# A graph-network edge stage on one core: its indirect gathers written out one by one, with the indices read in place

## The chip, the cores and the metric

One core of one Trainium2 chip runs the whole kernel in a single launch. The metric is the device time of a run in microseconds (us); the time before is the median of three runs. A profiled execution gives the instruction times that are read below. Engines are named as in the profile: PE (TensorE matmul), PEld (its weight load), DVE (VectorE), ACT (ScalarE), POOL (GpSimd), SP (SyncE, here the issuer of the plain DMAs).

## What is computed

Four graph layers over 1250 nodes of 512 features, with 21,250 edges sorted by their destination. Each layer's result is added to its input and layer-normalised. The first three use only sums over neighbours, which the kernel turns into products with a 1250 x 1250 matrix of edge counts. The fourth needs a message for each edge, and is the one that the change touches:

```python
def _L3_gnn_ref(x, edge_index, edge_attr, W1, b1, W2, b2, gamma, beta):
    src, dst = (edge_index[0], edge_index[1])
    msg = jax.nn.relu(x[src] + edge_attr)
    agg = jax.ops.segment_sum(msg, dst, num_segments=x.shape[0])
    h = x + agg
    h = jax.nn.relu(h @ W1 + b1) @ W2 + b2
    h = x + h
    mean = h.mean(axis=0)
    var = h.var(axis=0)
    h = (h - mean) * jax.lax.rsqrt(var + BN_EPS) * gamma + beta
    return h
...
x = _layernorm(x + _L3_gnn_ref(x, edge_index, edge_attr_512, ...), axis=-1)
```

## The kernel before

The program is one block per engine, with every wait written by hand as a semaphore count. Its stages follow each other: index preparation and counts (to about 120 us of the span), the three count-matrix layers (to about 380 us), the edge stage (380 to about 709 us), the second matrix of the last layer with batch norm, and the last layer norm with the store.

In the edge stage the edges are cut into `NG` = 42 groups of 512. A group is four edges (`TPG`) on each of 128 partitions. Groups are numbered g; rings of buffers hold them: `RING` = 6 slots of edge attributes (`ea`, 1 MB each) and `XRING` = 3 slots of gathered node rows (`xg`, also 1 MB). The program is seven rounds (`ITERS`) of six groups; round 0 is written out, later rounds are a hardware loop on the engines. For one group:

- **SP** loads 1 MB of attributes into `ea` (L355) once the scatter of the group six back has freed the slot; the first six loads are issued ahead (L330).
- **POOL** gathers the source rows. `gather` (L463 to L472) waits until the add of the group three back has freed the slot of `xg`, copies the group's 128 x 4 indices from the table `srcT_i` into a staging tile `idx4` (L467), waits for that copy, and issues four indirect DMAs (L471). Each of these fetches 128 rows of 2 KB from `x3_dram`, at the row numbers that stand in one column of the staging tile, into one quarter of the slot. The trace names the staging tile `idx` and the DRAM tensor `x_dram`.
- **DVE** adds, when the four gathers and the attributes have landed: `ea += xg` (L978), 128 x 2048 floats, both inputs in SBUF, and builds the one-hot window `hot_w` (L981). Every third group it adds a finished join into `preT` (L998), and once a round a block (L1005).
- **ACT** rectifies `ea` in place (L636), later copies the scatter's result to `zn` (L644) and the turned result to `zg` (L652).
- **PE** multiplies the one-hot window with the rectified rows (the scatter, L1311), transposes the result of the group before (the turn, L1322), and multiplies three groups at a time with the layer's first matrix (the join, L1332) or does a piece of the same product for the nodes themselves (the pre-block, L1296).

The table `srcT_i` (128 partitions x 42 x 4, int32, in SBUF) is written once by DVE at the start of the program, ahead of the count `idx_ready`, and never after. Ahead of the stage POOL waits for the stores of `x3_dram` and reads a flag; for irregular graphs it takes another path (L446 to L460), which these inputs don't take. Behind the stage, the last join must be added before ACT can rectify `preT` (L681) and PE can multiply with the second matrix (L1369).

The wait that frees a slot and the copy:

```python
if not (isinstance(g, int) and g < XRING):
    pool.wait_ge(add_done, g - XRING + 1)
pool.tensor_copy(idx4[:, slot, :], srcT_i[:, bass.ds(g, 1), :].rearrange("p a b -> p (a b)")).then_inc(idx_staged, 1)
pool.wait_ge(idx_staged, g + 1)
```

Of the kernel before, what the change touches and what calls it, by code (L numbers as in the profile page):

```python
# [37 lines left out]
NG = (E + GE - 1) // GE  # L38
# [9 lines left out]
RING = 6  # L48
# [4 lines left out]
XRING = 3  # L53
ITERS = NG // RING
# [14 lines left out]
def gnn_kernel(nc, x, src, dst, edge_attr, w01, b01, w02, b02, w11, b11, w12, b12, w2, b2,  # L69
               w31, b31, w32, b32, gamma, beta, out, x3_dram):  # L70
    with ExitStack() as ctx:
# [11 lines left out]
        def sb(name, shape, dtype):  # L83
            size = 2 if dtype in (BF16, F16) else 4
            n = 1
            for s in shape[1:]:
                n *= s
            return at(name, shape, dtype, place(n * size))

        def sem(name):  # L90
            return ctx.enter_context(nc.semaphore(name))
# [30 lines left out]
        a = r_a  # L122
# [7 lines left out]
        a = max(a, r_a + (KC * N * 4 + 2 * CH * 4 + 31) // 32 * 32)  # L130
# [63 lines left out]
        srcT_i = sb("srcT_i", [P, NG, TPG], I32)  # L194
        idx4 = sb("idx4", [P, XRING, TPG], I32)
# [47 lines left out]
        idx_ready = sem("idx_ready")  # L243
# [19 lines left out]
        blk_done, blk_added = sem("blk_done"), sem("blk_added")  # L263
        ea_loaded = [sem(f"ea_loaded{i}") for i in range(RING)]
        xg_loaded = [sem(f"xg_loaded{i}") for i in range(XRING)]
        idx_staged, idx_seen = sem("idx_staged"), sem("idx_seen")
        add_done, relu_done, win_ready = sem("add_done"), sem("relu_done"), sem("win_ready")
        scat_done, zn_ready, turn_done, zg_ready = sem("scat_done"), sem("zn_ready"), sem("turn_done"), sem("zg_ready")
        turn_seen = sem("turn_seen")
# [101 lines left out]
        def _(pool):  # L371
# [68 lines left out]
                pool.tensor_tensor(xn[0:rows(j), j, :], xn[0:rows(j), j, :], b2_b[0:rows(j), :], ALU.add).then_inc(xb_ready[2], 1)  # L440


            pool.wait_ge(x3_stored, 16 * NT)
            pool.wait_ge(agg_done[2], NCH * KC)
            irregular = pool.value_load(flag_i[0:1, 0:1], min_val=0, max_val=1)
# [14 lines left out]
                for r in range(TPG):  # L460
                    fix_load(NG - 1, r, edge_attr[(NG - 1) * GE + r:E:TPG, :])

            def gather(it, s):  # L463
                g, slot = RING * it + s, s % XRING
                if not (isinstance(g, int) and g < XRING):
                    pool.wait_ge(add_done, g - XRING + 1)
                pool.tensor_copy(idx4[:, slot, :], srcT_i[:, bass.ds(g, 1), :].rearrange("p a b -> p (a b)")).then_inc(idx_staged, 1)  # L467
                pool.wait_ge(idx_staged, g + 1)
                pool.sem_inc(idx_seen, 1)
                for r in range(TPG):  # L470
                    pool.indirect_dma_start(out=xg[:, slot, r, :], out_offset=None, in_=x3_dram[:, :],  # L471
                                            in_offset=bass.IndirectOffsetOnAxis(ap=idx4[:, slot, r:r + 1], axis=0)).then_inc(xg_loaded[slot], 16)  # L472

            for s in range(RING):
                gather(0, s)
            with pool.Fori(1, ITERS) as it:
                for s in range(RING):
                    gather(it, s)


        @block.scalar
# [927 lines left out]
```

## Time and profile before

| | |
|---|---|
| Time, median of 3 runs | 764.68 us (764.16 to 765.23) |
| Profiled execution | span 770.4 us, from its first to its last instruction; its time as a run is not listed apart from this |
| Busy, share of the span | PE 83%, PEld 53%, DVE 52%, POOL 50%, ACT 34% |
| Granted TensorE clock, mean | 0.922 of full speed |
| DMA | 103.09 MB, mean 134 GB/s |

A share of busy time is a mean over stages that have different limits, so the table alone doesn't tell what the edge stage waits for. The views used below are the chain of work that ended last (followed back from the last instruction, each step to what released it), the groups of instructions of one stretch with their idle time and its releaser, the timeline (start, duration, engine, line, operation, and in brackets the engine's idle time before it), the answer for one source line (shortest, median and longest duration), and the table of windows. A wait named "issue" is one in which the engine waited for nothing that the profile shows.

### The profile page before, as it was taken

What the parts mean: (1) busy time and instruction counts of PE and PEld (TensorE: products, weight loads), DVE (VectorE), ACT (ScalarE), POOL (GpSimd) and SP (SyncE); (2) the same over time, 40 slices, a digit from 0 to 9 for tenths busy, and PEclk for the clock granted to TensorE, in tenths of its full rate; (3) what the DMA queues carried; (4) which work ended last, traced back from release to release, by engine and by line L of the source; (5) the groups of instructions that cost most, each with busy time, mean ns of one, the idle gap of its engine ahead of it and who ended that gap; (6) DMA issues with size and microseconds to landing.
All of it is one profiled execution on the core that took longest, in us unless ns stands there. A gap on an engine that the chain in (4) does not pass through costs nothing.

```text
span 770.4 us, 9550 instructions
## 1 busy us (share of the span) xinstructions
PE 635.7 (83%) x2854; PEld 411.5 (53%) x2854; DVE 397.7 (52%) x765; ACT 262.4 (34%) x434; POOL 383.3 (50%) x401
## 2 busy tenths in 40 slices
PE   2597886998988988999886877988898978798963
PEld 1343335997888827988521333433354433345962
DVE  3798882766648492117443333434443434432767
ACT  1354442112463154111532423244333332343135
POOL 7388888201012038300177777777776777760000
PEclk9699997999999998999899899998999989999985
DMA  7600000000002000024568788877888788650003
GB/s 225 183 2 0 1 0 4 0 0 1 1 1 94 17 1 1 0 71 162 192 234 272 251 309 290 280 267 272 311 297 307 253 284 279 207 149 0 1 0 134
DMA packets 30332, 103.09 MB, mean 134 GB/s; under 512 B 6559, under 2 KB 7201, under 8 KB 24986
## 3 DMA queue, kind: packets, MB, share of 16 engines
q1 hardware_dynamic: 16858, 58.59, 21.4%
q0 software_dynamic: 13440, 44.05, 18.0%
q8 instruction: 20, 0.33, 0.2%
q14 instruction: 14, 0.11, 0.0%
HBM read 97.51 MB, written 5.12 MB: 133 GB/s over the span
## 4 chain that ended last, share of the span: by engine, by line
PE 33%; POOL 31%; issue 17%; DVE 9%; ACT 5%; DMA 3%; POOLq 1%; ACTq 0%; SPq 0%; DVEq 0%
POOL xg L471 25%; PE ps L1171 15%; PE ps L1196 8%; PE ps L1369 3%; POOL hot_lo L395 3%; POOL idx L467 2%; DVE stats L871 2%; DVE xn L891 2%; ACT countsT L563 2%; PE ps L1131 1%; DMA xg<-x_dram,idx 1%; PE ps L1146 1%; DMA row_src_i<-in_src_dram 1%; PE ps L1332 1%; PE ps L1311 1%
## 5 line engine op out<-in xcount | busy, mean ns | idle before, releaser
L471 POOL DMA_INDIRECT xg<-x_dram,idx x168 | 217.3, 1293 | 73.4 <-issue 40.2
L1311 PE MATMUL ps<-ea,hot_w 128*38 128x512 f32 x336 | 170.2, 654 | 50.6 <-ACT ea L636 50.5
L978 DVE TENSOR_TENSOR ea<-ea,xg 128x2048 f32<-128x2048 f32 x42 | 96.3, 2292 | 180.6 <-DMA xg<-x_dram,idx 180.6
L636 ACT ACTIVATE ea<-ea 128x2048 f32<-128x2048 f32 x42 | 80.2, 1910 | 186.9 <-DVE ea L978 186.9
L1311 PEld LDWEIGHTS ps<-ea,hot_w 128*38 128x38 f32 x336 | 38.3, 124 | 151.4 <-issue 95.2
L395 POOL TENSOR_SCALAR hot_lo<-iota_n,lo_col 128x128 bf16<-128x128 f16 x84 | 56.5, 683 | 8.6 <-POOL lo_col L391 8.6
L1131 PE MATMUL ps<-hot_code,hot_lo 128*128 128x380 bf16 x168 | 38.1, 353 | 20.3 <-POOL hot_lo L395 20.2
L777 DVE TENSOR_SCALAR hot_code<-iota_n,codeT 128x380 bf16<-128x380 f16 x168 | 52.6, 373 | 4.2 <-issue 3.8
L1332 PE MATMUL ps<-zg,w_s 128*128 128x114 f32 x448 | 53.6, 278 | 0.4 <-ACT zg L652 0.4
L467 POOL COPY idx<-srcT_i 128x4 int32 (+1 forms) x42 | 19.2, 456 | 66.9 <-issue 66.7
L1332 PEld LDWEIGHTS ps<-zg,w_s 128*128 128x128 f32 x448 | 51.1, 192 | 1.1 <-ACT zg L652 0.5
L1171 PE MATMUL ps<-counts,u_hi 128*128 x120 | 44.2, 369 | 6.4 <-issue 6.4
L1171 PE MATMUL ps<-counts,xs_hi 128*128 x120 | 44.5, 370 | 5.3 <-POOL xs_lo L434 5.3
L1131 PEld LDWEIGHTS ps<-hot_code,hot_lo 128*128 128x128 bf16 x168 | 15.9, 104 | 57.6 <-issue 44.6
L1146 PE MATMUL ps<-w_s,xT 128*128 128x512 f32 (+1 forms) x80 | 44.8, 644 | 0.0
L1171 PE MATMUL ps<-counts,u_lo 128*128 x120 | 43.9, 366 | 0.0
L1171 PE MATMUL ps<-counts,xs_lo 128*128 x120 | 43.8, 365 | 0.0
L553 ACT ACTIVATE std<-mv,eps_s 128x1 f32<-128x1 f32 x40 | 11.8, 295 | 75.0 <-DVE mv L873 75.0
L1105 PE MATMUL ps<-ident,xn 128*128 128x128 f32 (+1 forms) x120 | 20.1, 304 | 20.3 <-DMA xn<-in_x_dram 15.2
L429 POOL TENSOR_TENSOR g_lo<-g_f,g_hi 128x256 fp32r<-128x256 f32 (+1 forms) x10 | 7.5, 750 | 57.2 <-ACT g_f L576 57.2
L500 ACT ACTIVATE hot_abs<-iota_n,lo_col 128x128 bf16<-128x128 f16 x42 | 16.9, 402 | 50.8 <-POOL lo_col L391 50.8
L434 POOL TENSOR_TENSOR xs_lo<-xs_f,xs_hi 128x512 fp32r<-128x512 f32 (+1 forms) x10 | 12.7, 1270 | 40.3 <-ACT xs_hi L601 40.3
(193 smaller groups left out, 1092.7 us busy)
## 6 DMA issues: line engine op xcount, KB each, us to landing
ea<-in_edge_attr_dram SPq DMA_DIRECT2D x41, 1024.0 KB, 6.9
w_s<-in_L_gnn_W_dram SPq DMA_DIRECT2D x5, 1024.0 KB, 11.6
xg<-x_dram,idx POOLq DMA_INDIRECT x168, 5.3
xn<-in_x_dram SPq DMA_DIRECT2D x3, 768.0 KB, 13.1
x_dram<-xn SPq DMA_DIRECT2D x9, 256.0 KB
out_dram<-xn SPq DMA_DIRECT2D x9, 256.0 KB
w_s<-in_L_gnn_W_dram SPq DMA_DIRECT2D x2, 512.0 KB, 9.0
b_b<-in_L_gnn_b_dram SPq DMA_DIRECT2D x3, 256.0 KB, 5.6
```

The lines of the kernel that those rows point to most:

```text
L395: ins = pool.tensor_scalar(hot_lo[:, slot, r, :], iota_n[:, 0:P], lo_col[:, slot, r:r + 1], None, ALU.is_equal)
L467: pool.tensor_copy(idx4[:, slot, :], srcT_i[:, bass.ds(g, 1), :].rearrange("p a b -> p (a b)")).then_inc(idx_staged, 1)
L471: pool.indirect_dma_start(out=xg[:, slot, r, :], out_offset=None, in_=x3_dram[:, :], in_offset=bass.IndirectOffsetOnAxis(ap=idx4[:, slot, ...
L636: act.activation(ea[:, s, :, :], ea[:, s, :, :], ACT.Relu).then_inc(relu_done, 1)
L777: ins = dve.tensor_scalar(hot_code[:, slot, r, :], iota_n[:, 0:NCODE], codeT[:, bass.ds(g, 1), r:r + 1].rearrange("p a b -> p (a b)"), Non ...
L978: dve.tensor_tensor(ea[:, s, :, :], ea[:, s, :, :], xg[:, slot, :, :], ALU.add).then_inc(add_done, 1)
L1131: ins = pe.matmul(ps[:, 4 + slot, 0:NCODE], hot_lo[:, slot, r, :], hot_code[:, slot, r, :], start=(r == 0), stop=(r == TPG - 1))
L1146: ins = pe.matmul(ps[0:rows(j), 2 + j % 2, :], xT0[:, k, P * j:P * j + rows(j)], w01_s[:, k, :], start=(k == 0), stop=(k == KC - 1))
L1171: ins = pe.matmul(ps[:, cc, 0:CH], part[0:rows(j), j, P * cc:P * cc + P], rhs[0:rows(j), j, n], start=(m == 0), stop=(m == len(pairs) - 1))
L1196: ins = pe.matmul(ps[0:rows(j), 4 + n % 2, :], act_t[:, k, P * j:P * j + rows(j)], w[:, k, :], start=(m == 0), stop=(m == len(pairs) - 1))
L1311: ins = pe.matmul(ps[0:W, 4 + s % 2, :], hot_w[:, s, r, :], ea[:, s, r, :], start=(r == 0), stop=(r == TPG - 1))
L1332: ins = pe.matmul(join_bank(slot)[:, f, :, :].rearrange("p h w -> p (h w)"), w31_s[:, k, P * f:P * f + P], zg[:, slot, k, :, :].rearrange( ...
```

## The change

POOL's part of the edge stage is written out for all 42 groups. Each gather reads its column of indices from `srcT_i` itself instead of from `idx4`. The copy at L467, its semaphore `idx_staged`, the increment of `idx_seen` in this path and the loop over rounds are gone. The wait for the add of the group three back stays, now ahead of the first gather of a group, from the fourth group on. A wait for `idx_ready` is added ahead of the flag's load. `idx4` and `idx_seen` remain for the irregular path. No other engine's instructions change.

```diff
+            pool.wait_ge(idx_ready, 1)
             pool.wait_ge(x3_stored, 16 * NT)
             pool.wait_ge(agg_done[2], NCH * KC)
             irregular = pool.value_load(flag_i[0:1, 0:1], min_val=0, max_val=1)
...
-            def gather(it, s):
-                g, slot = RING * it + s, s % XRING
-                if not (isinstance(g, int) and g < XRING):
+            def gather(g):
+                slot = g % XRING
+                if g >= XRING:
                     pool.wait_ge(add_done, g - XRING + 1)
-                pool.tensor_copy(idx4[:, slot, :], srcT_i[:, bass.ds(g, 1), :].rearrange("p a b -> p (a b)")).then_inc(idx_staged, 1)
-                pool.wait_ge(idx_staged, g + 1)
-                pool.sem_inc(idx_seen, 1)
                 for r in range(TPG):
                     pool.indirect_dma_start(out=xg[:, slot, r, :], out_offset=None, in_=x3_dram[:, :],
-                                            in_offset=bass.IndirectOffsetOnAxis(ap=idx4[:, slot, r:r + 1], axis=0)).then_inc(xg_loaded[slot], 16)
-
-            for s in range(RING):
-                gather(0, s)
-            with pool.Fori(1, ITERS) as it:
-                for s in range(RING):
-                    gather(it, s)
+                                            in_offset=bass.IndirectOffsetOnAxis(ap=srcT_i[:, g, r:r + 1], axis=0)).then_inc(xg_loaded[slot], 16)
+
+            for g in range(NG):
+                gather(g)
```

How this moves POOL's instructions. The first piece is POOL before, at the head of the loop over rounds 1 to 6: one of the six groups in its body, and the register step to the next (`idx_125` is the staging tile).

```order
L476 UNCONDITIONAL_BRANCH
L476 ISA
L467 ISA [waits add_done]
L467 COPY idx_125<-srcT_i 128x4
L468 REGISTER_ALU
L471 DMA xg<-x_dram,idx_125 128x512 [waits idx_staged]
L471 DMA xg<-x_dram,idx_125 128x512 x3
L466 REGISTER_ALU
```

The second is POOL with the change, from the end of the irregular path into the stage.

```order
L454 DMA xg<-x_dram,idx_125 128x512 [waits fix_idx]
L456 DMA xg<-in_edge_attr_dram 64x512
L447 UNCONDITIONAL_BRANCH [waits fix_added]
L469 DMA xg<-x_dram,srcT_i 128x512 x12
L469 DMA xg<-x_dram,srcT_i 128x512 [waits add_done]
L469 DMA xg<-x_dram,srcT_i 128x512 x3
```

Before, a gather of each group waited for the copy's count and the copy's side for the add; now the first three groups are twelve gathers without a wait, and each of the 39 others is one gather that waits for the add and three that wait for nothing.

## Rows read from the trace of the kernel before

**Rows 1.** The page, chain that ended last: shares of the span by line.
```profile
POOL xg L471 25%; PE ps L1171 15%; PE ps L1196 8%; PE ps L1369 3%; POOL hot_lo L395 3%; POOL idx L467 2%; DVE stats L871 2%; DVE xn L891 2%; ACT countsT L563 2%; PE ps L1131 1%; DMA xg<-x_dram,idx 1%; PE ps L1146 1%; DMA row_src_i<-in_src_dram 1%; PE ps L1332 1%; PE ps L1311 1%
```
**Rows 2.** Groups of instructions by line, window 400 to 690 us; columns as named.
```profile
line engine op names shapes xcount | busy us, mean ns | idle before us <-releasers
L471 POOL DMA_INDIRECT xg<-x_dram,idx x158 | 205.9, 1303 | 68.7 <-issue 38.1 <-POOL idx L467 30.7
L1311 PE MATMUL ps<-ea,hot_w 128*38 128x512 f32 x312 | 159.3, 659 | 50.2 <-ACT ea L636 50.2
L978 DVE TENSOR_TENSOR ea<-ea,xg 128x2048 f32<-128x2048 f32 x40 | 91.7, 2292 | 175.0 <-DMA xg<-x_dram,idx 175.0
...
L1332 PE MATMUL ps<-zg,w_s 128*128 128x114 f32 x384 | 45.9, 278 | 0.0
...
L1296 PE MATMUL ps<-x3T,w_s 128*128 x173 | 23.8, 285 | 0.0
...
L1322 PE MATMUL ps<-ident,zn 38*128 38x38 f32 x156 | 17.1, 234 | 0.0
```
**Rows 3.** Timeline: POOL's first copy and gather, its last gather, DVE's last add.
```profile
380.71 0.19 POOL L467 COPY idx<-srcT_i 128x4 int32<-128x4 int32 x1 [66.71 <-issue]
...
381.83 1.18 POOL L471 DMA_INDIRECT xg<-x_dram,idx  x1 [0.93 <-POOL idx L467]
...
689.79 0.95 POOL L471 DMA_INDIRECT xg<-x_dram,idx  x1 [0.30 <-issue]
...
693.49 2.29 DVE L978 TENSOR_TENSOR ea<-ea,xg 128x2048 f32<-128x2048 f32 x1 [4.60 <-DMA xg<-x_dram,idx]
```
**Rows 4.** Answers for lines L471 and L467: duration ns min/median/max, first and last start us.
```profile
L471 POOL DMA_INDIRECT xg<-x_dram,idx x168: 942/947/3024, 381.8 to 689.8; - x168
L467 POOL COPY idx<-srcT_i x42: 187/191/2352, 380.7 to 683.9; 128x4 int32 x36, 128x4 int32<-128x4 int32 x6
```
**Rows 5.** Timeline: one group undisturbed on POOL, the next one's copy beside a DVE add.
```profile
447.43 0.20 POOL L467 COPY idx<-srcT_i 128x4 int32 x1
...
448.42 0.97 POOL L471 DMA_INDIRECT xg<-x_dram,idx  x1 [0.79 <-POOL idx L467]
...
449.69 0.94 POOL L471 DMA_INDIRECT xg<-x_dram,idx  x1 [0.30 <-issue]
...
452.88 2.29 DVE L978 TENSOR_TENSOR ea<-ea,xg 128x2048 f32<-128x2048 f32 x1 [7.29 <-DMA xg<-x_dram,idx]
453.13 2.09 POOL L467 COPY idx<-srcT_i 128x4 int32 x1
```
**Rows 6.** Timeline: a gather that starts beside a DVE add.
```profile
443.07 2.29 DVE L978 TENSOR_TENSOR ea<-ea,xg 128x2048 f32<-128x2048 f32 x1 [3.33 <-DMA xg<-x_dram,idx]
...
443.97 2.21 POOL L471 DMA_INDIRECT xg<-x_dram,idx  x1 [0.30 <-issue]
```
**Rows 7.** The page's costliest groups: the two lines over the whole span.
```profile
L471 POOL DMA_INDIRECT xg<-x_dram,idx x168 | 217.3, 1293 | 73.4 <-issue 40.2
...
L467 POOL COPY idx<-srcT_i 128x4 int32 (+1 forms) x42 | 19.2, 456 | 66.9 <-issue 66.7
```
**Rows 8.** Timeline: the one gather with a long gap before it.
```profile
589.50 0.95 POOL L471 DMA_INDIRECT xg<-x_dram,idx  x1 [2.12 <-issue]
```
**Rows 9.** DMA queues and issues, window 400 to 690 us.
```profile
q0 software_dynamic: 12579, 41.19, 44.7%
...
ea<-in_edge_attr_dram SPq DMA_DIRECT2D x35, 1024.0 KB, 6.9
xg<-x_dram,idx POOLq DMA_INDIRECT x158, 5.3
```
**Rows 10.** Windows: busy by engine, then granted clock, DMA share, GB/s.
```profile
575.00:600.00 25.00, 21.53 (x84) 9.08 (x82) 11.27 (x12) 7.67 (x9) 18.07 (x16) 0.93 0.85 301
...
377.00:692.00 315.00, 263.68 (x1083) 122.33 (x1082) 121.09 (x129) 115.64 (x130) 236.43 (x210) 0.92 0.80 269
...
603.00:610.00 7.00, 6.81 (x43) 4.50 (x41) 2.52 (x2) 1.07 (x1) 5.87 (x5) 1.00 0.99 370
```
**Rows 11.** Timeline: a group's scatter at full clock, and one in a slow stretch.
```profile
417.71 3.62 PE L1311 MATMUL ps<-ea,hot_w 128*38 128x512 f32 x8 [1.41 <-ACT ea L636]
...
426.68 6.30 PE L1311 MATMUL ps<-ea,hot_w 128*38 128x512 f32 x8 [4.98 <-ACT ea L636]
```

More of the change, by code:

```diff
@@ L265, in gnn_kernel @@
         xg_loaded = [sem(f"xg_loaded{i}") for i in range(XRING)]
-        idx_staged, idx_seen = sem("idx_staged"), sem("idx_seen")
+        idx_seen = sem("idx_seen")
         add_done, relu_done, win_ready = sem("add_done"), sem("relu_done"), sem("win_ready")
```

## The prediction

> **What bounds the kernel now.** I start with the chain of work that ended last, on the page. The PE matmuls lead it as a sum over all stages, but its largest single item is POOL's gather at L471, 25% of the span, and `POOL idx L467`, the copy that the change removes, has 2% [rows 1]. The reader is to see that both changed lines lie on the path. Then the edge stage alone. In the 290 us from 400 to 690, L471 is busy for 205.9 us, and DVE's add L978, its consumer, sits idle for 175.0 us until gathers land [rows 2]. PE, the next suspect, has the four rows of its scatter, join, pre-block and turn there: 159.3 + 45.9 + 23.8 + 17.1 = 246.1 us [rows 2]. The stage runs 42 groups. The first copy starts at 380.71 and the last group's starts at 683.9 [rows 3, 4], so a group takes 303.2 / 41 = 7.40 us, some 39.2 groups fall into the 290 us, and PE needs 6.28 us of each. POOL has all of the 7.40.
>
> The timeline of POOL shows why. In an undisturbed group the copy takes 0.19 us, the gather behind it starts 0.79 us after the copy's end, four gathers of about 0.95 us follow with 0.30 between them, and the next copy starts at once: 453.13 - 447.43 = 5.70 us [rows 5]. Nothing waits for a ring slot: the copy carries the wait for the adds and starts without a gap. The rest up to 7.40 is DVE. A gather that starts 0.90 us after DVE's add started takes 2.21 us, not 0.95, and ends 0.82 us after the add ends [rows 6]; a copy caught 0.25 us into an add takes 2.09 us, not 0.19, and ends with it [rows 5]. Both lines together hold 217.3 - 168 x 0.947 = 58.2 us and 19.2 - 42 x 0.191 = 11.2 us of this [rows 4, 7], together 69.4 us, 1.65 a group. Check: 5.70 + 1.65 = 7.35; one hole of 2.12 us between two gathers, 1.8 above the usual 0.30 [rows 8], and small change make the 7.40.
>
> **The change, part by part.**
> *Copy, semaphore round trip and register increment go.* Per group 0.19 + 0.79 = 0.98 us leave POOL. The gather behind a copy took 0.97 us where the others take 0.95, so 0.02 more.
> *The seam between groups.* Before, copy followed gather with no gap. Now gather follows gather, and the rows' price for that pair is 0.30 [rows 5]. It carries the wait for the add three groups back. Its bounds: 0.00, the gap at which the copy with that same wait started, and 0.79, the gap of the only gathers that carry any wait. I take 0.30, because the wait is long satisfied (the add of a group starts 2.8 us after its last gather ends in rows 3, and the slot is wanted two groups later), whereas behind the copy a count had just to arrive.
> Net per group: 0.98 + 0.02 - 0.30 = 0.70 us. 41 groups give 28.7. The first copy cost 0.19 + 0.93 before the first gather [rows 3]; the gather now takes its place, and I count 0.8 of these 1.12. Sum: **-29.5 us**.
> *Index read in place.* Each gather takes its 128 indices from `srcT_i` instead of `idx4`, both in SBUF, one int32 per partition. No row prices the first, the nearest is 0.947 [rows 4]; I take it unchanged. Bounds: the shortest gather, 942 ns (-0.8 us over 168), and, since three quarters of the gathers do no wait at all, 0.97 for all (+3.9 us).
> *Loop.* The undisturbed groups inside and the first ones outside it have the same gaps, so its removal is priced 0 beyond the above. 168 instructions in a row instead of 36 x 4 in a loop is little fetching. If a hole like the one of rows 8 came once for each fetch, three of them would be +5 us, the upper bound; the lower is the one hole gone, -1.8.
> *The wait for `idx_ready`* ahead of the flag's load: POOL passed the same count before its first one-hot. 0.
> *What stays: DVE's holds.* The copy's share does not leave with it, because whatever POOL starts during an add is held. The pieces of a group were 0.98, 1.27, 1.25, 1.25 and 0.95 apart and are now 1.25 apart, so the hold meets about the same distance to the next start: 0.58 us on average before (squares over twice 5.70), 0.63 now. That is 0.05 x 42 = 2 us less hold; I leave it out. The single values run from 1.0 to 2.1 us, but landings scatter the phase, so the mean of 42 should move by no more than 2 to 3 us either way.
>
> Under the sum, every piece hides nothing else on POOL, so each us is on the path as long as POOL stays the bound at 7.40 - 0.70 = 6.70 us a group. The next floors are PE with 6.28 us and the transfers. A group moves 4 x 41.19 / 158 MB of gathers and 1.05 MB of attributes [rows 9], 2.09 MB; at the 370 GB/s of the fastest 7 us that is 5.65 us, at the 301 GB/s of the fastest 25 us 6.95 [rows 10]. PE at 94% of its time will finish a little behind the last gather, where the join and the second layer wait for it: the last scatter before was already 0.5 us late behind a join. I add **+1.0 us**. Holds stand at 68 to 70 us as before.
>
> Sum: 770.4 - 29.5 + 1.0 = 741.9 us of span. The profiled span is 5.7 us above the median of 764.68 of the runs; I take the same difference off that median: **736.2 us**.
>
> **Holds and the notes.** The timeline of POOL in the stage has 36 gathers and 6 copies lengthened by over 1 us beside a DVE instruction with two SBUF inputs, each ending at a fixed distance behind it; one of each kind stands in [rows 5, 6]. The Trainium skill, "SBUF — State Buffer", section "Who interferes with whom", says that a `tensor_tensor` with two SBUF inputs contends with GpSimd's reads, but reports a probe in which it did not stall a DMA's descriptor generation. By that probe gathers would run free under the adds and only copies would be held, and the sum would be 11.2 us lower. This case's rows decide for the other reading, a gather of 2.21 us, and so I keep the whole hold.
>
> **Rivals.**
> *A, transfers become the pace.* For it: DMA engines are busy for 0.80 of the stage, 0.99 in its fastest 7 us, and no stretch of 25 us moved over 301 GB/s [rows 10]. Against: the 370 GB/s, and slots that are free two groups early. If 301 is all that lasts, a group takes 6.95 us, the gain is 42 x 0.45 = 19 us: 746 us. PE lagging by several us at the end gives the same side, 739 to 745.
> *B, the gather that waits pays 0.79.* 39 gathers x 0.49 = 19 us back: 755 us. For it: every gather that carries a wait now has 0.79. Against: its cause there is a count that has just been sent.
> *C, the copies' holds leave with them.* 736.2 - 11.2 = 725 us, the probe's reading above. Against: 36 of the 42 holds fell on gathers, so whatever starts next is held.
> *D, slower: PE's clock.* PE's granted clock is 0.92 in the stage [rows 10], and the scatter of a group takes 6.30 us in a slow stretch instead of 3.62 [rows 11]. At full clock PE would need about 6.28 x 0.92 = 5.8 us a group. If the mean fell below 5.8 / 7.40 = 0.78, PE would be slower than POOL was; at 0.75 a group takes 7.7 us, +0.3 x 42 = 13 us: 777 us. Against: the clock fell behind idle time (the 6.30 follows 4.98 us of idleness), and idle time shrinks here.
> *E, the change buys nothing*, because each gather that reads the large table costs 0.17 us more (29.5 / 168): 765 us. Nothing in the rows speaks for it.
>
> **How the numbers follow.** Forecast with its own range 730 to 741: 0.80. A 0.09, B 0.03, C 0.03, D 0.03, E 0.02. The bounds of the unknown terms (-0.8 to +3.9, -1.8 to +5, the seam -12 to +19, holds +-3) reach over the forecast to 729 and to 748, which takes in A; B, C, D and E lie outside. A measurement of this kernel tells a change from none at about 0.2%, 1.5 us. Faster by more: forecast, A, B, C, less a sliver, 0.94; same: half of E and that sliver, 0.02; slower: D, part of E and the unthought, 0.04.
>
> **What would show it.** Right: no copy in the stage; a gather every 1.25 us across groups, seams of 0.30; groups of 5.0 us when undisturbed and 6.7 on average; about 41 held gathers of 2 to 3 us, 68 to 70 us in all; first gather to last gather 280 us instead of 309; PE idle before the scatters much shortened; the stretch behind the last gather, 80 us, unchanged to 2 us. Seams of 0.8 mean B; under 60 us of holds mean C; waits for the add in front of gathers, with landings of 8 us and more, mean A; a granted clock under 0.8 means D; gathers of 1.1 us without an add beside them mean E. A time above 748 or below 729 refutes the sum.

## The result and the profile after

The changed kernel takes 734.39 us, median of four runs (733.16 to 739.25), against 764.42 us (764.15 to 765.23) for the kernel before in the same comparison: a ratio of 0.962, 95% interval 0.958 to 0.967. That is 30.0 us less; 28.5 were forecast from the median known then, and 736.2 us as the time.

The page of the changed kernel, chain and costliest groups (out<-in xcount | busy us, mean ns | idle before, releaser):

```profile
POOL xg L469 29%; PE ps L1166 16%; PE ps L1191 8%; PE ps L1364 3%; POOL hot_lo L395 3%; DVE stats L866 2%; PE ps L1126 2%; DVE xn L886 2%; ACT countsT L558 2%; PE ps L1141 2%; DMA row_src_i<-in_src_dram 1%; PE ps L1327 1%; PE ps L1306 1%; PE ps L1231 1%; ACT hT L683 1%
...
L469 POOL DMA_INDIRECT xg<-x_dram,srcT_i x168 | 222.0, 1322 | 117.3 <-issue 117.3
L1306 PE MATMUL ps<-ea,hot_w 128*38 128x512 f32 x336 | 159.4, 619 | 26.3 <-ACT ea L631 26.3
L973 DVE TENSOR_TENSOR ea<-ea,xg 128x2048 f32<-128x2048 f32 x42 | 96.3, 2292 | 145.4 <-DMA xg<-x_dram,srcT_i 145.4
```

The copy has left the chain that stood in [rows 1], and the gather is still its largest item: 29% of a shorter span, because nearly all that left was between gathers. POOL is still the engine that sets the pace. PE's wait for rectified rows before the scatter, 50.6 us on the page before, is 26.3 now. The line for the gathers, as in [rows 4]:

```profile
L469 POOL DMA_INDIRECT xg<-x_dram,srcT_i x168: 942/946/2999, 378.8 to 650.8; - x168
```

A gather that reads its index column in the big table takes 946 ns in the median, 947 before. The timeline of POOL across the seam between two groups (400.88 is the last gather of one, 402.13 the first of the next), to be held against [rows 5]:

```profile
399.62 0.95 POOL L469 DMA_INDIRECT xg<-x_dram,srcT_i  x1 [0.30 <-issue]
400.88 0.95 POOL L469 DMA_INDIRECT xg<-x_dram,srcT_i  x1 [0.30 <-issue]
402.13 0.95 POOL L469 DMA_INDIRECT xg<-x_dram,srcT_i  x1 [0.30 <-issue]
403.38 0.95 POOL L469 DMA_INDIRECT xg<-x_dram,srcT_i  x1 [0.30 <-issue]
404.63 2.46 POOL L469 DMA_INDIRECT xg<-x_dram,srcT_i  x1 [0.30 <-issue]
```

The reader sees a flat train at 1.25 us in which the group's border has disappeared, and at 404.63 a gather held beside an add. All 41 seams are 0.30 or 0.31 us. The two ends of the stage, as in [rows 3], and the windows, as in [rows 10] (busy by engine, clock, DMA share, GB/s):

```profile
378.83 1.18 POOL L469 DMA_INDIRECT xg<-x_dram,srcT_i  x1 [66.41 <-issue]
```
```profile
650.79 0.95 POOL L469 DMA_INDIRECT xg<-x_dram,srcT_i  x1 [0.30 <-issue]
...
654.54 2.29 DVE L973 TENSOR_TENSOR ea<-ea,xg 128x2048 f32<-128x2048 f32 x1 [4.65 <-DMA xg<-x_dram,srcT_i]
```
```profile
377.00:660.00 283.00, 256.67 (x1114) 123.44 (x1114) 123.71 (x131) 116.15 (x129) 222.02 (x168) 0.96 0.84 298
```

From POOL's first instruction of the stage to the end of its last gather it is 651.7 - 378.8 = 272.9 us now, and was 690.7 - 380.7 = 310.0. From there to the end of the span it is 79.7 us in both. The granted clock in the stage went from 0.92 [rows 10] to 0.96 (the third number from the end of the window's line).

The two profiled spans differ by 39.0 us, the medians by 30.0. The run profiled for the rows before was a long one: its holds were 69.4 us and its mean group 7.40 us, where experiment 1 below, the same staged gathers, has 62.5 and 7.23. So some 7 us of holds belong to that execution. The hole of [rows 8], 1.8 us above the usual gap, is not in this profile either; which profiles have it is told in the last section. The medians give the gain.

Words used below: a *hold* is what a gather or copy takes above its usual time beside a DVE instruction; a *seam* is the gap between the last gather of one group and the first of the next; a *group* is measured from its first gather to the next group's first gather, and the mean group is over the 41 such stretches of a profile.

### The profile page after: what moved, and what is told of

The parts are those of the page before. It is cut to its first block, busy times and chain, and to the rows that moved or that the text cites. A ratio compares the mean times of both kernels' runs of the same rounds, so it can differ in the third digit from the quotient of the medians.

```text
span 731.4 us, 9369 instructions
## 1 busy us (share of the span) xinstructions
PE 621.8 (85%) x2854; PEld 408.6 (56%) x2854; DVE 398.3 (54%) x765; ACT 262.5 (36%) x434; POOL 368.5 (50%) x359
## 4 chain that ended last, share of the span: by engine, by line
PE 35%; POOL 34%; issue 13%; DVE 9%; ACT 6%; DMA 2%; POOLq 1%; ACTq 0%; SPq 0%; DVEq 0%
POOL xg L469 29%; PE ps L1166 16%; PE ps L1191 8%; PE ps L1364 3%; POOL hot_lo L395 3%; DVE stats L866 2%; PE ps L1126 2%; DVE xn L886 2%; ACT countsT L558 2%; PE ps L1141 2%; DMA row_src_i<-in_src_dram 1%; PE ps L1327 1%; PE ps L1306 1%; PE ps L1231 1%; ACT hT L683 1%
## 5 line engine op out<-in xcount | busy, mean ns | idle before, releaser
L469 POOL DMA_INDIRECT xg<-x_dram,srcT_i x168 | 222.0, 1322 | 117.3 <-issue 117.3
L1306 PE MATMUL ps<-ea,hot_w 128*38 128x512 f32 x336 | 159.4, 619 | 26.3 <-ACT ea L631 26.3
L1306 PEld LDWEIGHTS ps<-ea,hot_w 128*38 128x38 f32 x336 | 36.4, 118 | 117.9 <-issue 88.0
L1141 PE MATMUL ps<-w_s,xT 128*128 128x512 f32 (+1 forms) x80 | 44.5, 639 | 0.0
L1317 PEld LDWEIGHTS ps<-ident,zn 38*128 38x128 f32 x168 | 13.5, 138 | 34.4 <-issue 34.3
L434 POOL TENSOR_TENSOR xs_lo<-xs_f,xs_hi 128x512 fp32r<-128x512 f32 (+1 forms) x10 | 12.7, 1271 | 38.4 <-ACT xs_hi L596 38.4
```

Of the source, the lines that this page charges most:

```text
L1141: ins = pe.matmul(ps[0:rows(j), 2 + j % 2, :], xT0[:, k, P * j:P * j + rows(j)], w01_s[:, k, :], start=(k == 0), stop=(k == KC - 1))
L1306: ins = pe.matmul(ps[0:W, 4 + s % 2, :], hot_w[:, s, r, :], ea[:, s, r, :], start=(r == 0), stop=(r == TPG - 1))
```

## The experiments

Each was timed beside the kernel before on its own chip, and the ratio to that is given too. Experiments 1 to 4 ran on one chip, 5 to 8 on a second, 9 to 12 on a third, with medians of 762.4, 763.7 and 762.9 us for the kernel before. The chip matters more than these figures let one think, as experiment 9 and the last section show. Four-run medians scatter by 1 to 3 us.

**1. The loop written out, the copy kept.**

```diff
-            for s in range(RING):
-                gather(0, s)
-            with pool.Fori(1, ITERS) as it:
-                for s in range(RING):
-                    gather(it, s)
+            for g in range(NG):
+                gather(g // RING, g % RING)
```

> The kernel before, with POOL's loop over rounds written out, the staging copy and its wait kept. My theory (the gain is all in the copy and the round trip behind it): undisturbed groups stay at 5.70 us, seams between gathers of two groups at 0.98, the time at 764 us within 1.5. Rival (the loop, its register steps and branches cost something of the 30 us): undisturbed groups under 5.6 us and a time under 760 us.

Measured: 763.9 us against 762.4, ratio 1.002 (0.999 to 1.005). Undisturbed groups take 5.69 to 5.71 us, and 0.98 us pass between the last gather of a group and the first of the next when nothing holds the copy. The two lines of POOL:

```profile
L471 POOL DMA_INDIRECT xg<-x_dram,idx x168 | 206.1, 1227 | 73.7 <-issue 49.2 <-POOL idx L467 24.5
L467 POOL COPY idx<-srcT_i 128x4 int32<-128x4 int32 x42 | 23.6, 561 | 66.9 <-issue 66.6
```

The loop was free: the interval leaves it at most 4 us either way, and the undisturbed group didn't change at all. So the gain is the staging. The holds here are 206.1 - 168 x 0.947 = 47.0 us on gathers and 23.6 - 42 x 0.192 = 15.5 us on copies. In the changed kernel there are no copies, and its gathers carry 222.0 - 168 x 0.946 = 63.1 us: the copies' share moved to the next gather to within a us.

**2. A copy put back, but not waited for.**

```diff
+                pool.tensor_copy(idx_all[:, g, :], srcT_i[:, g, :])
                 for r in range(TPG):
                     pool.indirect_dma_start(out=xg[:, slot, r, :], out_offset=None, in_=x3_dram[:, :],
```

> The changed kernel, with a copy of the group's indices put back on POOL ahead of each group's gathers, into a tile that nobody reads, and no wait for it. My theory (the copy costs its 0.19 us, the wait for its count the other 0.5): the gather behind a copy starts 0.30 us after it, undisturbed groups take 5.2 us, the time is 734.4 + 42 x 0.19 = 742 us, 740 to 745. Rival (any gather behind another POOL instruction starts 0.79 us late, waited for or not): undisturbed groups at 5.70 us and a time of 760 to 765 us.

Measured: 739.8 us (737.5 to 742.6), ratio 0.973 (0.967 to 0.979), against 734.4 to 735.8 us for the changed kernel. Undisturbed groups take 5.10 us. POOL's timeline at a seam:

```profile
417.30 0.94 POOL L471 DMA_INDIRECT xg<-x_dram,srcT_i  x1 [0.30 <-issue]
418.25 0.20 POOL L469 COPY idx_all<-srcT_i 128x4 int32<-128x4 int32 x1
418.61 0.98 POOL L471 DMA_INDIRECT xg<-x_dram,srcT_i  x1 [0.16 <-issue]
```

The copy fits into the 0.30 us that stand before any gather and adds 0.06 there, with the longer gather behind it 0.1 a group. So the 0.70 us that each group lost consist of some 0.1 for the copy and 0.6 for waiting until its count came back. (The increment of `idx_seen`, which also went, is inside these 0.6; no run parts the two.) The expectation had the copy's own price too high (0.19), hence 740 at best where 739.8 was measured.

**3. Most of the add taken away**, to remove the holds. The add covers one of four row blocks.

```diff
-                dve.tensor_tensor(ea[:, s, :, :], ea[:, s, :, :], xg[:, slot, :, :], ALU.add).then_inc(add_done, 1)
+                dve.tensor_tensor(ea[:, s, 0, :], ea[:, s, 0, :], xg[:, slot, 0, :], ALU.add).then_inc(add_done, 1)
```

> The changed kernel, whose add on DVE covers only the first of the four gathered rows of each partition; three quarters of the gathered rows are fetched and left out of the sum. My theory (the gathers are lengthened by the add beside them and by nothing else): holds fall from 63 us in all to under 10, undisturbed groups stay at 5.0 us, POOL could go at 5.1 us a group, and PE with 5.8 to 6.0 us a group sets the pace: 734.4 - 42 x 0.55 - 1.7 at the end = 708 to 714 us, POOL's gathers finishing early or waiting for adds. Rival A (transfers already set the pace): groups stay at 6.3 us or more, time over 725 us, landings longer. Rival B (gathers are lengthened for another reason, for instance by the transfers in flight): holds stay at 50 to 60 us and the time at 731 to 735 us.

Measured: 741.7 us, ratio 0.975 (0.969 to 0.981), slower than the changed kernel although DVE has less to do. The part of the theory on holds is right: gathers are busy for 166.1 us in all, against 168 x 0.947 = 159.1, so the holds are 7 us where they were 63. The part on the time is wrong. Who waits for whom from 400 to 640 us (us, times, longest), and one cycle of the timeline:

```profile
DVE preT L993 <- remote: 138.7, 9, 15.8
...
POOL xg L469 <- DVE ea L973: 51.9, 11, 8.0
```
```profile
499.95 1.21 DVE L993 TENSOR_TENSOR preT<-preT,ps 128x152 f32 x3 [15.11 <-remote]
...
501.08 0.68 DVE L973 TENSOR_TENSOR ea<-ea,xg 128x512 f32<-128x512 f32 x1
...
502.04 1.38 POOL L469 DMA_INDIRECT xg<-x_dram,srcT_i  x1 [4.68 <-DVE ea L973]
...
510.75 3.83 PE L1327 MATMUL ps<-zg,w_s 128*128 128x114 f32 x32
...
516.24 0.95 POOL L469 DMA_INDIRECT xg<-x_dram,srcT_i  x1 [0.30 <-issue]
...
519.44 1.21 DVE L993 TENSOR_TENSOR preT<-preT,ps 128x152 f32 x3 [15.79 <-remote]
```

POOL now issues twelve gathers without a break (502.04 to 517.2), then stops for 4 us; DVE adds three groups in a burst, then stands for 15 us until a join is done. PE's join matmuls end at 514.6 in the profile (whose matmul ends are modelled), yet DVE is released only at 519.4. Three groups take 19.4 us, 6.4 to 6.5 each; over the stage the mean group is 6.37 us. The profile calls the releaser "remote", so it doesn't know it; by the program it is PE's count of the finished join, and the trace's own record of that count stands at 519.31, 4.7 us behind the end of the matmuls.

The gathers themselves were through sooner than in the changed kernel: 265.8 us from the start of the first to the end of the last, against 272.9. The time was lost behind them. PE ended its last scatter 22.2 us after the last gather (669.9 against 647.7), and 11.3 us after it in the changed kernel (663.0 against 651.7); 90.6 us remain to the end of the span instead of 79.7. A group of 6.3 us or more and a time over 725 us were rival A's figures, but the transfers were not at their floor: this version moved 319 GB/s in the middle of the stage and experiment 9 moved more.

**4. The add in four pieces.**

```diff
-                dve.tensor_tensor(ea[:, s, :, :], ea[:, s, :, :], xg[:, slot, :, :], ALU.add).then_inc(add_done, 1)
+                for r in range(TPG):
+                    ins = dve.tensor_tensor(ea[:, s, r, :], ea[:, s, r, :], xg[:, slot, r, :], ALU.add)
+                ins.then_inc(add_done, 1)
```

> The changed kernel, with DVE's add in four pieces of 512 columns, back to back, behind the same wait. My theory (a hold lasts to the end of the one DVE instruction that POOL meets, then POOL gets its turn): no gather over 1.6 us, holds of 0.3 us on average and about two of them a group, 0.5 to 0.7 us a group instead of 1.5; POOL at 5.6 us a group, PE at about 6.0: 712 to 722 us. Rival A (back-to-back pieces keep POOL out until the last one): gathers of 2 to 3 us as before and 733 to 738 us. Rival B (a gather in progress holds up DVE's next piece): pieces start up to 0.8 us late, the adds get slower, and the time stays over 728 us.

Measured: 767.9 us in the median of eight, 756 to 773; no ratio was worked out. That is no better than the kernel before. Gathers are busy for 181.1 us in all, so the holds did fall to 22 us, and nearly all single ones are under 0.5 us, as a hold that ends with the DVE instruction it meets should be. Three gathers stand out with 4.1 to 4.4 us above the usual, each held through the pieces of two adds that follow each other. The bursts are there again: POOL waits up to 11.2 us for an add, DVE up to 17.3 us for a join. The pieces start back to back and take 0.69 us each, so a gather in progress doesn't hold them up. This expectation failed as the one before it did, in what follows when POOL gets ahead.

**5. PE lightened alone**: the scatter takes three of four row blocks.

```diff
-                for r in range(TPG):
-                    ins = pe.matmul(..., start=(r == 0), stop=(r == TPG - 1))
+                for r in range(TPG - 1):
+                    ins = pe.matmul(..., start=(r == 0), stop=(r == TPG - 2))
```

> The changed kernel, whose scatter multiplies three of the four row blocks of a group; a quarter of the messages is left out of the sum, and PE has about 0.9 us less to do in each group. Theory (POOL still sets the changed kernel's pace: gathers at 1.25 us and one hold): mean group stays within 0.15 us of 6.49, the time falls by 1 to 3 us at the end of the stage alone, 731 to 734 us. Rival (PE's 6.0 to 6.4 us a group already sets it): the mean group falls under 6.2 us and the time to 722 us or less.

Measured: 728.4 us (726.7 to 732.7), ratio 0.953 (0.947 to 0.959). The mean group is 6.56 us. PE had less to do and the groups didn't get shorter: POOL sets the changed kernel's pace, as forecast; all 41 seams are again 0.30 or 0.31 us, so POOL never waited. PE's load fell by less than a quarter of the scatter, though: the scatter is busy for 137.2 us instead of 159.4, which is 0.5 us a group and not 0.9, because the granted clock in the stage is 0.91 here and 0.96 there, and a matmul of it takes 688 ns instead of 619. The time is some 6 us lower than the changed kernel's, between the two expectations. The profiled run is the slowest of the four (732.7 us), and neither its groups nor the end of its stage show the 6 us, so they aren't explained.

**6. Both lightened.** The edits of 3 and 5 together.

> Both at once: the add covers a quarter and the scatter three quarters (these parts of the sum are left out). Theory (with the holds gone, PE's work is the floor, which is why the quarter add alone took 741.7 us): groups fall to between 5.65 us (370 GB/s) and 6.06 us (345 GB/s), where the transfers end it; 697 to 714 us. Rival (not PE's work but the handshake does: DVE waits for a join of two groups ago and POOL for three slots, in bursts): the burst pattern and a time of 735 to 742 us stay.

Measured: 733.0 us, ratio 0.959 (0.952 to 0.965). The bursts stay: DVE's adds come as three within 2 us and then none for 17 to 18, and a mean group is 6.45 us, 6.37 in 3, though PE's scatter is busy for 0.6 us less a group (130.0 us in all against 155.9). The rival holds in its mechanism: in 3 it was not PE's work that set the length of a group. Its time (735 us or more) was a little too high, and the ratio is 0.016 below that of 3. Of that the profiles show some 5 us behind the last gather, where PE had less left to do (85.2 us instead of 90.6), and 5 us before the stage, where the two programs are the same.

**7. An add for each gather, and the join taken later.** Each gather got its own semaphore, each add of 512 columns waits for its own, and the join and block adds moved one group back in DVE's order.

```diff
-                    if s % JOIN == 0 and not (isinstance(it, int) and it == 0):
+                    if s % JOIN == 1 and not (isinstance(it, int) and it == 0):
...
-                    if s == 1 and not first:
+                    if s == 2 and not first:
```

> The changed kernel with two alterations: a semaphore for each gather and four adds of 512 columns, each as soon as its gather has landed, and DVE takes a finished join and block one group later than before. Theory (single short adds spread over the group hold POOL for 0.1 us each on average, and the later join keeps DVE from standing still): POOL at 5.4 us a group, PE at 6.2 to 6.4 sets the pace: 724 to 731 us, faster than the changed kernel. Rival (POOL runs ahead until the ring stops it and then idles, as with the add in four pieces): waits of POOL for adds of 5 us and more, 740 us or more.

Measured: 772.5 us (768.2 to 779.9), ratio 1.015 (1.006 to 1.023), the slowest. Holds are 25 us, POOL waits up to 12.7 us for an add, DVE up to 20.1 us for a join. The rival's pattern, worse than it said.

**8. The later join alone.**

> The changed kernel, with DVE taking a finished join and block one group later. Theory (DVE waited for joins for 0.3 us in all in the changed kernel, so there is nothing to win): 732 to 737 us. Rival (the early join holds adds up often enough to matter in runs that weren't profiled): 730 us or less.

Measured: 733.6 us, ratio 0.961 (0.954 to 0.969): no difference from the changed kernel, as expected.

**9. The quarter add again, and POOL kept from running ahead.** It waits for the add two groups back, so that it is at most eight gathers ahead of the adds instead of twelve.

```diff
-                if g >= XRING:
-                    pool.wait_ge(add_done, g - XRING + 1)
+                if g >= 2:
+                    pool.wait_ge(add_done, g - 1)
```

> As the quarter add (three quarters of the gathered rows are left out of the sum), but POOL waits for the add of the group two back instead of three back, so that it can run ahead by 8 gathers at most. Theory (what ended the groups at 6.4 us there was POOL's running ahead: rows piled up in the queues, and PE's counts of finished joins came up to 8 us late): the three-group bursts go, joins are seen within 1 us, groups go at PE's pace of about 6.0 us: 718 to 728 us. Rival (the transfers' 330 GB/s or PE's work are the floor whatever POOL does): groups stay at 6.3 us or more, 735 us or more.

Measured: 713.8 us (709.3 to 718.3), ratio 0.938 (0.930 to 0.947), better than the 718 to 728 expected and 28 us less than experiment 3. Waits from 400 to 630 us, and windows of the middle, this kernel first, then experiment 3:

```profile
DVE ea L973 <- DMA xg<-x_dram,srcT_i: 157.9, 36, 8.8
...
POOL xg L469 <- DVE ea L973: 41.4, 26, 4.2
...
DVE preT L993 <- issue: 17.5, 11, 1.8
...
DVE preT L993 <- PE ps L1327: 2.6, 1, 2.6
```
```profile
500.00:550.00 50.00, 50.00 (x243) 25.79 (x242) 11.38 (x27) 22.15 (x27) 32.03 (x34) 1.00 0.97 353
550.00:600.00 50.00, 50.00 (x229) 24.21 (x228) 11.66 (x28) 22.94 (x25) 32.62 (x35) 1.00 0.97 363
```
```profile
500.00:550.00 50.00, 48.28 (x221) 24.20 (x220) 10.92 (x28) 22.50 (x27) 30.31 (x31) 0.97 0.89 319
```

Before a join's sum DVE stands for 1.8 us at most, once 2.6, and 9.3 for a join behind the last gather; POOL's waits are 26 short ones instead of 11 long ones. The mean group is 5.95 us, PE is busy for the whole 50 us at full clock, and the transfers move 353 to 363 GB/s. PE sets the pace here, at 5.9 to 6.0 us a group, with the transfers close behind.

How much of the 28 us the stricter wait gave is not shown, because the chip changed with it. In every profile from the third chip, the changed kernel's among them, PE's counts of finished joins come within 0.05 us of the end of the matmuls. In every profile from the first two chips some come late, even where POOL waits as in the changed kernel (last section). The quarter add with the old wait was not run on the third chip.

**10. The full add in four pieces, POOL two back.** The edits of 4 and 9.

> As the add in four pieces, with POOL waiting for the add two groups back. Theory (short holds are worth 0.9 us a group once POOL doesn't run ahead): 720 to 730 us, faster than the changed kernel. Rival (the shorter ring makes POOL wait for adds in most groups, and that costs what the holds give): 735 to 750 us.

**11. The changed kernel, POOL two back.**

> The changed kernel with only this: POOL waits for the add two groups back. Theory (an add starts about 5 us after its last gather ends and takes 2.3, against 6.5 us for the group between, so in every second or third group POOL waits a little): 1 to 3 us of waits for adds in such groups, 740 to 760 us. Rival (slots are free in time with two as with three): 733 to 737 us.

**12. The changed kernel again.**

> The changed kernel once more, on the chip of these runs: 732 to 738 us, undisturbed groups of 5.0 us, seams of 0.30, mean group 6.45 to 6.6 us.

Measured on one chip: 733.2 us for 10 (ratio 0.961, 0.953 to 0.968), 750.9 for 11 (0.990, 0.980 to 0.999), 735.8 for 12 (0.966, 0.959 to 0.973). The add in four pieces, which in experiment 4 gave back the whole gain, is now level with the changed kernel, and perhaps 2.7 us ahead, within the scatter of either; here too the chip changed along with the wait. The 720 to 730 expected for 10 were missed: the holds fell to 9 us, but POOL waits 61.4 us for adds from 400 to 640 us, as the rival said. In 11, POOL waits 44.5 us for adds in 230 us, because with the long add the second slot isn't free in time; the expectation had 1 to 3 us a time and got 0.5 to 4.6. So the tighter ring costs 15 us with the long add, on the same chip; that it pays with short ones is likely and not shown. Experiment 12 gives the changed kernel's figures once more: undisturbed groups of 5.0 us, mean group 6.54, holds 222.3 - 159.1 = 63.2 us. No version was found that is clearly faster than the changed kernel and computes the same.

## Why the prediction was right

- **The bound.** POOL's train of copy, round trip and gathers set the pace. What left the train left the time, us for us, and in the changed kernel POOL waits for nothing in all 41 seams. In 5, less work on PE left the mean group at 6.5 us.
- **The seam.** 0.30 us was taken between bounds of 0.00 and 0.79; all 41 are 0.30 or 0.31. A wait that is long satisfied costs a gather nothing. Rival B, the 0.79, is out.
- **Copy and round trip**, 0.98 + 0.02 - 0.30 = 0.70 us a group: an undisturbed group went from 5.70 to 5.00. Experiment 2 divides it, 0.1 for the copy and 0.6 for the wait.
- **Indices in place**: 946 against 947 ns. **The loop**: 0, by experiment 1. Rival E is out.
- **Holds stay.** They were to be "68 to 70 us as before" and are 63.1 and 63.2; 40 gathers are lengthened by over 1 us, where about 41 were forecast. The size was taken from one long execution; the staged program has 62.5 in experiment 1. That they don't leave with the copies is shown by these 62.5 us with copies and 63.1 without, so rival C is out, and with it the reading by which gathers would run free beside a `tensor_tensor`: taking three quarters of the add away took 56 of 63 us off the gathers.
- **+1.0 us for PE behind the last gather** is not seen in the first profile: 79.7 us before and after. The last groups came 7 us apart (holds again), and PE had caught up. In the profile of experiment 12 it is there: PE began its last scatter at 662.28, though its rows were rectified at 659.34, and ended it 13.2 us behind the last gather instead of 11.3, so 1.9 us later; in all, 82.9 us remain behind that gather. So the mechanism is real and comes or doesn't with the last few groups; one profile doesn't size it.
- **The mean group**: 6.70 forecast, 6.49 and 6.54 measured. The forecast started from the 7.40 of the long execution; from the 7.23 of experiment 1 it would have been 6.53.
- **The time**: 0.70 x 42 = 29.4 us came off the median of 764.4, and the median gain is 30.0. The forecast of 736.2 was 1.8 us high, most of it the 1.0 us for PE. The holds stand on both sides of the change, so their wrong size cost the sum nothing.
- **Rivals A and D** did not occur: POOL never waited for an add in the changed kernel, and the clock rose. But A's side was nearer than it looked. In experiment 9 PE is busy throughout, at 5.9 us a group from 500 to 600 us where the prediction had 5.8 at full clock, and the transfers move 353 to 363 GB/s there.

## What to carry to other kernels

Where an engine issues transfers back to back and is the bound, price a small staging copy by the wait behind it, not by its own length: here 0.1 us against 0.6, 42 times. Before taking work away from a neighbour to speed up such a train further, ask what its ring lets it run ahead by: in the changed kernel POOL never met the end of its three slots, and with the short add it ran into it every twelve gathers and the whole became slower. When a comparison is to show a cure, run both sides on one chip: the 28 us between experiments 3 and 9 can't be divided between the wait and the chip. And look at more than one execution before taking a mean of irregular stalls from it: the 5.70 us of an undisturbed group was exact, the 7.40 us mean was not.

## What the runs showed of the hardware

PE's counts of finished joins arrived late in some profiles. The delay is taken from the end of a join's last matmul to the trace's record of its count. The largest of each profile:

| Profiles | Chip | Largest delay, us |
|---|---|---|
| before, changed | not on record | under 0.05 |
| 9, 10, 11, 12 | third | under 0.05 |
| 1, 2 (waits as before or as changed) | first | 1.0, 1.6 |
| 5, 8 (waits as changed) | second | 4.3, 2.8 |
| 3, 4 (POOL gets ahead) | first | 7.7, 7.8 |
| 6, 7 (POOL gets ahead) | second | 8.2, 13.0 |

In experiment 3 ten counts are 4 to 8 us late, and each of them comes 1.8 to 2.4 us after the end of the twelfth gather in a row; DVE then starts its sum, up to 7.9 us after the join (8.4 in experiment 6). So two things go with the size of the delay: the chip, and whether POOL gets ahead until the ring stops it. All versions with the stricter wait ran on the third chip, where the changed kernel has no delay either, so that limiting the run-ahead cures it is not shown. By what a count is held is open. That rows landed late isn't shown either: the profiles of 1 to 8 give no times of landing.

The long gap of [rows 8] is before the second gather of group 28. A gap above 0.4 us stands at that same gather, the 114th, in nine of the fourteen profiles: 2.12 us in the kernel before and in experiment 1, 0.59 in 3, 4, 6, 9, 10 and 11, and 0.87 in 12, whatever the time at which it is issued. The first profile of the changed kernel and experiments 2, 5, 7 and 8 have none. That it always is the 114th speaks for something that counts gathers, not time; nothing was run on it.

Back-to-back adds can keep POOL out for longer than one of them: 4.1 to 4.4 us above the usual in three gathers of experiment 4, where four pieces of one add follow those of another.
